# A decoder layer on one core: the end of the projection moves into the attention's first slot, and the ring of score banks turns at cell 16

## The reference

```
q = lin(lin(x, wq, bq), vq, bvq); k, v likewise       # two linear layers each, 512 -> 512
q, k, v -> 32 heads of 16 columns, for each of 4 batches
scores = q k^T / 4;  attn = softmax(scores);  o = attn v
x = layernorm(x + lin(o, wo))
x = layernorm(x + gated_cell(causal_conv(x), ctx, z0))   # kernel size 2, four gates
x = layernorm(x + ternary_ffn(quantised(x)))
```

## Time and profile before

| | us |
|---|---|
| median of 3 runs (lowest, highest) | 2087.46 (2086.99, 2290.2) |
| the profiled execution | 2087.88 |
| its span | 2086.2 |
| TensorE busy | 2033.5 (97%) |
| VectorE busy | 1644.6 (79%) |
| ScalarE busy | 1318.8 (63%) |
| GpSimd busy | 487.9 (23%) |

### The profile page before, as it was taken

One profiled execution on the slowest core, in us unless ns is written; L12 is line 12 of the kernel. 1 busy time (PEld: TensorE's weight loads), 2 busy tenths in 40 slices (PEclk: granted clock), 3 DMA queues, 4 the chain that ended last, 5 costly groups with the idle time before them and its releaser, 6 DMA issues.

```text
span 2086.2 us, 42029 instructions
## 1 busy us (share of the span) xinstructions
PE 2033.5 (97%) x12280; PEld 1160.1 (56%) x12280; DVE 1644.6 (79%) x1727; ACT 1318.8 (63%) x2429; POOL 487.9 (23%) x878
## 2 busy tenths in 40 slices
PE   9999999999999999999999999999999999999996
PEld 4788775444444444444444444444444487767774
DVE  4333356999999999999999999999999467886687
ACT  0112113888888888888888888888888743453344
POOL 0000001112212221221122122212211462464245
PEclk9999998999999999999999999999999999999997
DMA  4455835566675765776665757667757678763672
GB/s 166 138 164 150 197 109 110 85 131 134 108 136 120 120 135 99 137 139 106 129 133 106 138 118 120 131 106 137 139 103 168 225 258 322 286 228 121 230 265 96
DMA packets 214415, 315.26 MB, mean 151 GB/s; under 512 B 105424, under 2 KB 121808, under 8 KB 202064
## 3 DMA queue, kind: packets, MB, share of 16 engines
q1 hardware_dynamic: 214352, 314.47, 62.8%
HBM read 211.06 MB, written 101.19 MB: 150 GB/s over the span
## 4 chain that ended last, share of the span: by engine, by line
PE 89%; DVE 6%; ACT 1%; DMA 1%; issue 1%; POOL 1%; SPq 0%; POOLq 0%; DVEq 0%; ACTq 0%
PE psum L549 25%; PE psum L187 23%; PE psum L574 19%; PE psum L223 12%; PE psum L585 7%; PE psum L88 2%; DVE stats L1448 1%; PE psum L1368 1%; DVE y L1573 1%; ACT probs L672 1%; DVE gates L1547 1%; DVE gates L1544 1%; ACT gates L1297 1%; DMA x_block<-in_x_t_dram 0%; DVE y L1478 0%
## 5 line engine op out<-in xcount | busy, mean ns | idle before, releaser
L230 DVE TENSOR_REDUCE neg_max<-psum 128x1 f32<-128x1024 f32 x1024 | 1195.0, 1216 | 116.6 <-PE psum L223 100.0
L672 ACT ACTIVATE probs<-psum 128x512 f32<-128x512 f32 x2048 | 1069.4, 602 | 236.0 <-PE psum L549 232.7
L549 PE MATMUL psum<-q_op,k_op 50*128 50x512 f32 x2048 | 693.0, 452 | 3.8 <-ACT probs L672 3.3
L223 PE MATMUL psum<-k_op,q_op 48*128 48x512 f32 x2048 | 664.8, 491 | 0.4 <-DVE neg_max L230 0.3
L549 PEld LDWEIGHTS psum<-q_op,k_op 50*128 50x128 f32 x2048 | 337.1, 191 | 511.0 <-ACT probs L672 489.2
L574 PE MATMUL psum<-probs,v_op 128*32 128x512 f32 x3080 | 412.8, 608 | 9.3 <-issue 7.1
L223 PEld LDWEIGHTS psum<-k_op,q_op 48*128 48x128 f32 x2048 | 405.3, 315 | 13.4 <-DVE neg_max L230 5.2
L187 PE MATMUL psum<-x_wino,conv_w 128*128 128x512 f32 x1152 | 276.0, 395 | 0.2 <-DMA conv_w<-conv_w_parts_dram 0.2
L187 PEld LDWEIGHTS psum<-x_wino,conv_w 128*128 128x128 f32 x1152 | 214.5, 188 | 46.3 <-issue 0.6
L241 POOL CAST neg_max_parts<-neg_max 128x8 fp32r<-128x8 f32 x128 | 24.5, 192 | 740.2 <-DVE neg_max L230 740.2
L585 PE MATMUL psum<-probs,v_op 128*32 128x256 f32 x2032 | 163.2, 393 | 0.0
(11 more groups left out here) (105 smaller groups left out, 1707.4 us busy)
## 6 DMA issues: line engine op xcount, KB each, us to landing
q_op<-qk_parts_dram SPq DMA_DIRECT2D x384, 128.0 KB, 4.8
conv_w<-conv_w_parts_dram SPq DMA_DIRECT2D x32, 1536.0 KB, 6.7
qk_parts_dram<-qk_parts SPq DMA_DIRECT2D x128, 256.0 KB, 3.2
k_op<-qk_parts_dram SPq DMA_DIRECT2D x384, 64.0 KB, 4.9
conv_w_parts_dram<-conv_w_parts SPq DMA_DIRECT2D x16, 1536.0 KB, 7.0
attended_dram<-out SPq DMA_DIRECT2D x64, 256.0 KB, 2.8
attended_parts_dram<-o_parts SPq DMA_DIRECT2D x128, 128.0 KB, 3.6
gates<-in_ctx_dram SPq DMA_DIRECT2D x32, 512.0 KB, 7.5
```

What stands on the lines that cost most here:

```text
L223: return nc.tensor.matmul(mem["pair"][t % 2][:, lane * HALF:(lane + 1) * HALF], ops["q"][i][r, b, t:S:QT], ops["k"][i][r, b, :], start=Tru ...
L230: nc.vector.tensor_reduce(ops["max"][b][:, t:t + 1], mem["pair"][t % 2][:], AX_X, ALU.max, negate=True).then_inc(ops["maxed"], 1)
L549: nc.tensor.matmul(score_bank(k, t, last), kop[k][r, j // 2, n // 2 * P:(n // 2 + 1) * P], qop[k][r, j // 2, j % 2 * HALF:(j % 2 + 1) * HALF],
L672: nc.scalar.activation(probs[n % DEEP][:, c ^ n % 2, :], score_bank(k, t, last), ACT.Exp, scale=SCALE).then_inc(exp_done, 1)
```

## The change

`KEPT = 2`: the last two value groups of the last block, and the last two lead units with their maxima, leave the projection. TensorE computes them in slot 0 of the attention: each kept group is cut into two pieces of six matmuls, and pieces and lead units stand between the first cells and units of the slot (`kept_values`, `lead_unit`). The groups go into bank 7, one after the other, and VectorE takes them out between maxima (`kept_out`: the first between maxima 22 and 23, the second behind maximum 25). The waits at the head of the attention, on TensorE, SP and GpSimd, are lowered by two groups. TensorE's first attended values of slot 0 wait for all value copies. Since the kept groups need x's and the values' weights, x's second pair of parts, the third pair of weights and the value bias are placed in memory where the attention puts nothing in its first slot.

The ring: cell c of a turn uses bank c % 3 below cell 16 and (30 - c) % 3 from there on, so that the order of the banks is mirrored at cell 16 (14 and 16 share a bank, 13 and 17, 12 and 18). The wait of each cell is worked out from the distance to the cell that used its bank last (`since`), and the order of the wide banks follows.

The diff:

```diff
--- before.py
+++ after.py
@@ -191,6 +191,7 @@
 
 LEAD = 3 * QT
 PROJECTED = N // HALF * 3 * KC
+KEPT = 2
 OPS = 12 * DMA
 MAXES = 2 * PARTS * DMA
 
@@ -303,7 +304,7 @@
                     qk0 = (it * 2 + i) * (2 * KC)
                     v0 = (it * 2 + i) * KC
                     pe.wait_ge(x_made, it * 2 + i + 1)
-                    for j in range(GROUPS):
+                    for j in range(GROUPS - (KEPT if units and i == 1 else 0)):
 
                         if j < BANKS:
                             pe.wait_ge(v_out, v0 + j + 1)
@@ -364,7 +365,7 @@
 
             for blk in range(BLK):
                 i, beta = blk % 2, blk // (BLK // 2)
-                for j in range(GROUPS):
+                for j in range(GROUPS - (KEPT if blk == BLK - 1 else 0)):
                     if j < 2 * KC:
                         dve.wait_ge(qk_hi, blk * (2 * KC) + j + 1)
                         nc.vector.scalar_tensor_tensor(
@@ -397,13 +398,15 @@
                 split_max(nc, pool, ops, n // 2, n % 2, n, n * QT + QT)
 
 
-def attend(nc, block, sem, mem, qk_scr, v_sb, us_scr, r_scr, on_scr, cw_scr, wo_t, conv_w, x_nat, wo_b, tern_t, norm, late, ops, proj, qk_lo, v_out):
+def attend(nc, block, sem, mem, qk_scr, v_sb, us_scr, r_scr, on_scr, cw_scr, wo_t, conv_w, x_nat, wo_b, tern_t, norm, late, ops, proj, qk_lo, v_out, kept):
 
     STEPS = QT
     TILES = 4
     RING = 3
     DEEP = 4
     WIDE_FROM = 2 * STEPS + 5
+    TURN = 16
+    KEPT_OUT = (1,)
     EVACUATE_AFTER = 8
     with ExitStack() as ctx:
         sb = lambda name, shape, dt: ctx.enter_context(nc.sbuf_tensor(name, shape, dt))
@@ -419,7 +422,7 @@
         wide = sb("conv_w_parts", [P, 3, PARTS, KC * P], F32R)
         bank = mem["banks"]
         s2_bank = [bank[4], bank[5], bank[6]]
-        wide_bank = s2_bank + [bank[0], bank[1], bank[2]]
+        wide_bank = [s2_bank[0], s2_bank[2], s2_bank[1], bank[0], bank[1], bank[2]]
         pv_bank = bank[7]
 
         op_in, max_in, ones = ops["in"], ops["max_in"], ops["ones"]
@@ -444,17 +447,26 @@
             sp.dma_start(taps[:], conv_w[bass.ds(w, 1), :, :, :].rearrange("a p (t c) n -> p (a t) (c n)", t=2))\
                 .then_inc(taps_in, DMA)
 
+        def turning(cell):
+
+            return (cell if cell < TURN else 2 * TURN - 2 - cell) % RING
+
+        def since(cell):
+
+            cells = 4 * STEPS * TILES
+            return next(d for d in range(1, cells) if turning((cell - d) % cells) == turning(cell))
+
         def score_bank(k, t, last):
 
             cell = k * (STEPS * TILES) + t
             wide = cell - WIDE_FROM * TILES
             if last and wide >= 0:
                 return wide_bank[wide % (2 * RING)]
-            return s2_bank[cell % RING]
+            return s2_bank[turning(cell)]
 
         @block.sync
         def _(sp):
-            sp.wait_ge(proj, PROJECTED)
+            sp.wait_ge(proj, PROJECTED - KEPT)
             sp.wait_ge(ones, 5)
             load_op(sp, qk_scr, ops, 2, 2)
             load_taps(sp, 0)
@@ -528,7 +540,7 @@
         def _(pe):
             pe.wait_ge(ones, 4)
             pe.wait_ge(qk_lo, 8 + PROJECTED // 3 * 2)
-            pe.wait_ge(v_out, 4 + PROJECTED // 3)
+            pe.wait_ge(v_out, 4 + PROJECTED // 3 - KEPT)
 
             def shifted(it, k, t, last):
 
@@ -545,7 +557,7 @@
                 elif last and wide >= 2 * RING:
                     pe.wait_ge(exp_done, it * 4 * (STEPS * TILES) + cell + 1 - RING)
                 else:
-                    pe.wait_ge(exp_done, it * 4 * (STEPS * TILES) + cell + (2 if cell < 2 else 1))
+                    pe.wait_ge(exp_done, it * 4 * (STEPS * TILES) + cell + RING + 1 - since(cell))
                 nc.tensor.matmul(score_bank(k, t, last), kop[k][r, j // 2, n // 2 * P:(n // 2 + 1) * P],
                                  qop[k][r, j // 2, j % 2 * HALF:(j % 2 + 1) * HALF],
                                  start=True, stop=True).then_inc(s2_full, 1)
@@ -568,6 +580,8 @@
                 if n == 0:
                     pe.wait_ge(v_ready, s + 1)
                     pe.wait_ge(pv_out, s + 1)
+                    if k == 0:
+                        pe.wait_ge(v_out, 4 + PROJECTED // 3)
                 pe.wait_ge(exp_done, s * (STEPS * TILES) + n * TILES + TILES + RING)
                 for j in range(TILES):
                     kt = n // 2 + QT // 2 * ((n + j) % 2)
@@ -587,6 +601,24 @@
                 if half == 1:
                     mm.then_inc(pv_step, 1)
 
+            def lead_unit(n, lane):
+
+                pe.wait_ge(maxed, n - 1)
+                b, t = n // QT % 2, n % QT
+                score_lane(nc, mem, ops, n // 16, b, t, lane)
+                score_lane(nc, mem, ops, n // 16, b, t, 1 - lane).then_inc(s1_full, 1)
+
+            def kept_values(m, kcs):
+
+                if m > 0 and kcs[0] == 0:
+                    pe.wait_ge(v_out, 4 + PROJECTED // 3 - KEPT + m)
+                cols = slice((KC - KEPT + m) * P, (KC - KEPT + m + 1) * P)
+                mm = product3(nc, pv_bank, [(kept["xh"][:, kc, cols], kept["xl"][:, kc, cols],
+                                             kept["wh"][:, kc, :], kept["wl"][:, kc, :]) for kc in kcs],
+                              kcs[0] == 0, kcs[-1] == KC - 1)
+                if kcs[-1] == KC - 1:
+                    mm.then_inc(proj, 1)
+
             def slot(it, k, first=False, last=False):
                 s = it * 4 + k
 
@@ -606,20 +638,39 @@
 
                 for n in range(0, STEPS, 4):
                     t, u = n * TILES, 2 * n
-                    shifted(it, k, t, last)
-                    shifted(it, k, t + 1, last)
-                    half_at(n - 2, 0)
-                    shifted(it, k, t + 2, last)
-                    unit(it, k, u, 1, last)
-                    shifted(it, k, t + 3, last)
-                    shifted(it, k, t + 4, last)
-                    unit(it, k, u + 1, 1, last)
-                    half_at(n - 2, 1)
-                    shifted(it, k, t + 5, last)
-                    shifted(it, k, t + 6, last)
-                    shifted(it, k, t + 7, last)
-                    unit(it, k, u + 2, 0, last)
-                    values_at(n - 1)
+                    if first and k == 0 and n == 0:
+                        shifted(it, k, 0, last)
+                        shifted(it, k, 1, last)
+                        kept_values(0, (0,1))
+                        lead_unit(LEAD - 2, 0)
+                        shifted(it, k, 2, last)
+                        kept_values(0, (2,3))
+                        lead_unit(LEAD - 1, 1)
+                        shifted(it, k, 3, last)
+                        unit(it, k, 0, 0, last)
+                        shifted(it, k, 4, last)
+                        kept_values(1, (0,1))
+                        unit(it, k, 1, 1, last)
+                        shifted(it, k, 5, last)
+                        kept_values(1, (2,3))
+                        shifted(it, k, 6, last)
+                        shifted(it, k, 7, last)
+                        unit(it, k, 2, 0, last)
+                    else:
+                        shifted(it, k, t, last)
+                        shifted(it, k, t + 1, last)
+                        half_at(n - 2, 0)
+                        shifted(it, k, t + 2, last)
+                        unit(it, k, u, 1, last)
+                        shifted(it, k, t + 3, last)
+                        shifted(it, k, t + 4, last)
+                        unit(it, k, u + 1, 1, last)
+                        half_at(n - 2, 1)
+                        shifted(it, k, t + 5, last)
+                        shifted(it, k, t + 6, last)
+                        shifted(it, k, t + 7, last)
+                        unit(it, k, u + 2, 0, last)
+                        values_at(n - 1)
                     shifted(it, k, t + 8, last)
                     unit(it, k, u + 3, 1, last)
                     shifted(it, k, t + 9, last)
@@ -691,7 +742,19 @@
                     if n == 2 and k % 2 == 1 and not (first and k == 1):
                         recips(dve, nc, norm, it * 2 + (k - 3) // 2)
                     max_of_unit(nc, dve, mem, ops, 1 - n // QT, n % QT, s * 16 + n + LEAD)
-
+                    if first and k == 0 and n in KEPT_OUT:
+                        kept_out(1)
+
+            def kept_out(m):
+
+                dve.wait_ge(proj, PROJECTED - KEPT + m + 1)
+                nc.vector.tensor_tensor(
+                    kept["values_of"][:, :, 1, :, 4 * KC - KEPT + m, :], pv_bank.rearrange("p (g h d) -> p g h d", g=2, d=DH),
+                    kept["bias"].rearrange("p (g h d) -> p g h d", g=2, d=DH), ALU.add).then_inc(v_out, 1)
+
+            max_of_unit(nc, dve, mem, ops, 0, QT - 2, LEAD - 2)
+            kept_out(0)
+            max_of_unit(nc, dve, mem, ops, 0, QT - 1, LEAD - 1)
             for k in range(4):
                 slot(0, k, first=True)
             with dve.Fori(1, LAST) as it:
@@ -734,7 +797,7 @@
                 pool.wait_ge(taps_lo, w + 1)
```

(24 more changed lines are left out.)

## The result

The changed kernel takes 2070.39 us (median of 4 runs, 2069.09 to 2072.35) against 2087.22; the ratio is 0.9923, interval 0.9903 to 0.9942. The forecast was 2070.9. The profiled execution took 2069.09 us against 2087.88.

What follows compares the result with a forecast made beforehand. VectorE's maxima, then half-rate TensorE bound the seam; TensorE's waits nearly everywhere behind. Seam 3.3 + clock 6.7 + ring 6.8 - 0.2 = 16.6 us off 2087.88, less 0.42 to the median: 2070.9 us, range 2066.5 to 2078.2.

Steps and rivals of the forecast that it cites:

- The clock: First to fifth attended values of slot 0: TensorE's clock holds at full rate, 6.7 us go; fall rival 15 in 100.
- My comparison of 16 matmuls in 3.9 us with 29 in 3.4: TensorE's issue before the clock fell at the old seam, set against a full-rate stretch, to call the seam thin.
- The ring: Loop passages: mirroring banks at cell 16 ends cell 1's stall, 0.45 x 15, 6.8 us, bounds 4 and 9.
- the loop's jump: Passage between loop turns: 0.15 of its 0.6 us was left to the jump, which stays.
- Cell 16's slack of 0.26 us: Weights load after cell 14's exponential, so the short distance costs nothing; rival that it stalls, 8 in 100.
- The seam: Tenth value group's end to first attended values: these start at 343.3, not 346.6, gain 3.3 us, bounds 1.9 and 4.2.
- The replay: Working for the seam from 332.1 us: VectorE's new order of copies and maxima, maximum 26 ending at 342.7.
- SP's late maxima: Slot 1's third score waits for SP's loads: 0.2 us charged, bounds 0 and 1.4; rival 6 in 100.
- the slower rival: Slot 0 and following: clock falls behind the seam and stays down; 2095 us at 60 us cold; 4 in 100.

Runs made afterwards that it cites:

- The fill: Kernel before plus 24 full matmuls, their result overwritten, between the first cells and units of slot 0: 2084.59 us, ratio 0.9977.
- thin: Changed kernel with one matmul in place of six in each of the four kept pieces, so the layer isn't computed: 2070.49 us.
- units alone: Changed kernel, but the last two value groups stay in the projection and only the two lead units move: 2075.82 us, ratio 0.9939.
- the starved slots: Changed kernel with one, two or four extra unused VectorE maxima ahead of slot 2's fifth unit: 2070.36, 2075.78 and 2078.51 us.
- whole: Changed kernel with each kept group in one piece of twelve matmuls, in place of two of six: 2071.36 us.
- after: The changed kernel with both parts, seam and ring: median 2070.39 us, profiled execution 2069.09 us.
- before: The kernel without the change: median 2087.22 us, profiled execution 2087.88 us.
- slot 2: Changed kernel with four extra unused VectorE maxima in a row ahead of the fifth unit of slot 2: 2078.51 us.
- Two extra maxima: Changed kernel with two extra unused VectorE maxima (2.3 us) ahead of the fifth unit of slot 2: 2075.78 us.

## Why the prediction was right, step by step

- **The clock, 6.7 us: right** in mechanism and size (16.83 to 10.13). The fill, thin, units alone and the starved slots show it from four sides: TensorE work put into the seam keeps the clock up, and taking it away, or making TensorE wait elsewhere, lets it fall. How thin is too thin they don't show: whole held with 14 matmuls in 3.9 us. My comparison of 16 matmuls in 3.9 us with 29 in 3.4 "of the same kind of work" was not a fair one either, since 16 of those 29 are matmuls of attended values, of which the seam had none.
- **The ring, 6.8 us predicted, 9.0 measured: mechanism right, term too small**, at its upper bound of 9. I left 0.15 us of each passage to the loop's jump; in after only 0.04 are left of it (10.25 + 10.17 against the 10.31 + 10.07 of ordinary half slots in before), so nearly the whole cost of a passage was the ring's, 0.59 by the turns. Cell 16's slack of 0.26 us held: no wait there.
- **The seam, 3.3 us predicted, 1.2 measured: the step of the working that failed**, below even its lower bound of 1.9. The replay followed VectorE and let TensorE be early; in the trace of after the chain from 331.85 to 344.33 is TensorE's alone. I had priced the kept groups at 5.81, their price among their own kind. Between score matmuls a piece of six takes 1.60, so 6.4 us for the four, and the unit behind a piece 0.56 where one in an ordinary half slot takes 0.24. VectorE in turn stood still 0.59 us ahead of each of the two copies, for products that came later than in my replay; I had allowed 0.3 for one:

```profile
336.50 0.69 DVE L751 TENSOR_TENSOR values<-psum,v_bias 128x512 f32<-128x512 f32 x1 [0.59 <-PE psum L187]
...
341.52 0.69 DVE L751 TENSOR_TENSOR values<-psum,v_bias 128x512 f32<-128x512 f32 x1 [0.59 <-PE psum L187]
```

  These rows are VectorE's in order of time, in after. The two errors, 2.1 too much here and 2.2 too little in the ring, cancelled, which is luck: the total, 0.5 us from the median, was closer than its terms.
- **SP's late maxima, 0.2 us: not needed.** The series ran as forecast, without a gap and some 0.8 us earlier, since the whole seam stood 1.1 us earlier in this execution. GpSimd's and SP's rows in order of time, in after:

```profile
331.10 1.84 POOL L802 MEMSET k_op<- 128x1024 f32 x2 [15.16 <-PE psum L187]
...
332.17 0.36 SPq L207 DMA_DIRECT2D q_op<-qk_parts_dram  x1
...
350.77 2.52 SPq L217 DMA_DIRECT2D q_op<-neg_max_parts  x4
```

  The four stores land 4.8 us from issue (median), the last at some 357.6. The third score of slot 1 comes at 359.07, later than forecast with the seam, so 1.4 us were to spare.
- **What I got wrong about the slower rival**: I reckoned with a cold stretch that repeats what was seen, 20 us or more. In the traces it was 20.5 at the old seam in three kernels, but 10.2 in thin and 13.7 in slot 2.

## What to carry to other kernels

Where a clock dip stands behind a stage change, look at what TensorE does in the microseconds ahead of it, try a fill of useless matmuls as a probe, and move real work there; the wait itself may be worth a microsecond and the dip seven. Don't take a count of matmuls from one dip for a limit. When you replay a seam, follow both engines, and price a matmul by rows that have its neighbours, not its kind. Where banks rotate over a loop whose length isn't a multiple of the ring, put the short distances where the reader of the bank is ahead, and measure the excess over a whole turn.

## What the runs showed that I had not expected

- Two extra maxima, a wait of 1.7 us in the trace, cost some 7 us in five of nine executions of one kernel and nothing in the other four. With one, a wait of 0.6 us, four of five stood at mean clocks of 0.991 and 0.992 and the fifth at 0.989 (2072.8 us); with four, a wait of 4.0 us, five of six stood at 0.988 and the sixth at 0.991.
- Once at half clock, TensorE was busy nearly without a break, and the clock took 20.5 us to come back at the old seam, 13.7 in slot 2, 10.2 in the thin kernel. What decides between these I did not find; no run was made for it. Each is the length in one profiled execution; the other four runs of thin have mean clocks of 0.985 to 0.989 against its 0.990, so theirs may have been longer.
- The finish isn't the same in each execution, though nothing in it was changed. Between 1850 and 1910 us the clock stood at half in three stretches of 3.4, 3.4 and 6.8 us in the trace of before, and in one of 3.4 in that of after, and still the finish as a whole differs by 0.8 us only. So two executions are compared by stretches, not by mean clock.
